# Layer 2's output, layer 3's norm and layer 3's table of messages and keys in one phase of seven node groups

## The reference, cut to what matters

```python
h = jnp.maximum(_layernorm(x), 0.0)
x = x + _L2_gnn_ref(h, edge_index, edge_weight, edge_weight_n2)    # a weighted segment sum
h = jnp.maximum(_layernorm(x), 0.0)
x = x + _L3_gnn_ref(h, ...)

# in _L3_gnn_ref, for an edge of type r from node s:
rel_emb = W_r.mean(axis=-1)[edge_type]                              # 64 values for each of 8 types
key_base = x_src @ Wk1 + rel_emb @ Wk2 + Wk_bias
key_rule = rule_emb[rule_ids] @ Wk3
msg = x_src @ W_r[r]
```

## Time and profile before

| what | us |
|---|---|
| median of 3 runs | 7159.0 |
| lowest and highest | 7148.41 and 7164.03 |
| the profiled execution, its own time | 7143.65 |
| its span in the trace | 7141.9 |
| from the first transpose of `out2` to the first instruction after `table3` | 114.6 (4956.14 to 5070.71) |

### The profile page before, as it was taken

How to read it: one execution, slowest core, us unless ns; L and a number is a source line. 1 busy time by engine, 2 the same in 40 slices (tenths; PEclk the granted TensorE clock), 3 DMA queues, 4 the chain that set the end, 5 groups by cost and what they waited for, 6 DMA issues and landing times. The chain is left out here.

```text
span 7141.9 us, 137103 instructions
## 1 busy us (share of the span) xinstructions
PE 4348.4 (61%) x28781; PEld 2978.7 (42%) x28782; DVE 4343.3 (61%) x20718; ACT 3028.4 (42%) x9954; POOL 5254.0 (74%) x5903
## 2 busy tenths in 40 slices
PE   3343333443356666666666659997777777777774
PEld 2333333333344332323333337776455555555552
DVE  4333333333326666666666679998676666666667
ACT  1000000000004555555555547775466666666663
POOL 6777777777736777777777759997477777777773
PEclk6555555555557767677667679998777777777776
DMA  4333333333325666666666647774533333333331
GB/s 135 100 101 99 103 103 103 101 97 102 103 51 156 169 170 169 170 170 169 169 170 170 169 143 236 240 240 157 189 80 79 79 79 79 79 79 78 79 79 46
DMA packets 657986, 909.22 MB, mean 127 GB/s; under 512 B 141822, under 2 KB 424512, under 8 KB 657537
## 3 DMA queue, kind: packets, MB, share of 16 engines
q1 hardware_dynamic: 480886, 599.15, 26.9%
q0 software_dynamic: 175648, 308.58, 18.8%
q10 hardware_dynamic: 1357, 0.47, 0.0%
HBM read 697.55 MB, written 210.23 MB: 127 GB/s over the span
## 5 line engine op out<-in xcount | busy, mean ns | idle before, releaser
L827 POOL DMA_INDIRECT rows<-src_rows,idx_slots x1568 | 1499.9, 957 | 541.3 <-issue 476.4
L827 POOL DMA_INDIRECT rows<-node_rows,idx_slots x1568 | 1504.2, 959 | 505.9 <-issue 473.9
L827 POOL DMA_INDIRECT rows<-rel_rows,idx_slots x1568 | 1486.1, 948 | 486.3 <-issue 451.6
L1252 PE MATMUL bank<-onehot,ones 128*128 128x512 f32 x1568 | 1242.4, 887 | 10.6 <-ACT onehot L1261 10.6
L1261 ACT ACTIVATE onehot<-ident,fresh_slots 128x128 f32<-128x128 f32 x3136 | 989.3, 386 | 38.4 <-DVE fresh_slots L1388 33.9
L1077 DVE TENSOR_TENSOR wide_room<-bank,wide_room 96x128 f32 x392 | 112.6, 287 | 1326.7 <-PE bank L1055 1326.3
L1041 ACT ACTIVATE rows<-edge_in 128x128 f32<-128x128 f32 x392 | 120.7, 309 | 1836.2 <-PE bank L1055 1820.0
L1349 PE MATMUL bank<-w_e,edge_in 128*128 128x256 f32 x784 | 402.5, 609 | 750.3 <-DVE onehots L906 704.3
L1055 PE MATMUL bank<-onehot,rows 128*96 128x128 f32 x1568 | 390.2, 431 | 628.3 <-issue 328.5
L1055 PE MATMUL bank<-onehots,rows 128*96 128x128 f32 x1568 | 393.9, 433 | 588.7 <-issue 529.7
L1349 PEld LDWEIGHTS bank<-w_e,edge_in 128*128 128x128 f32 x784 | 167.1, 264 | 1248.5 <-DVE onehots L906 782.7
(11 more groups left out here) (274 smaller groups left out, 10192.6 us busy)
## 6 DMA issues: line engine op xcount, KB each, us to landing
edge_in<-dst_line SPq DMA_DIRECT2D x392, 256.0 KB
spill<-rows SPq DMA_DIRECT2D x392, 256.0 KB
rows<-spill SPq DMA_DIRECT2D x392, 256.0 KB, 3.0
hot_rows<-rows SPq DMA_DIRECT2D x98, 712.0 KB, 3.7
onehots<-hot_rows SPq DMA_DIRECT2D x98, 712.0 KB, 4.3
onehots<-src_low SPq DMA_DIRECT2D x98, 512.0 KB, 6.3
edge_in<-in_ea_l SPq DMA_DIRECT2D x98, 256.0 KB, 4.1
rows<-node_rows,idx_slots POOLq DMA_INDIRECT x1568
```

Source lines behind the costliest of these rows:

```text
L827: pool.indirect_dma_start(out=to[:, b.slot(ROW_RING), g, :], out_offset=None, in_=table, in_offset=bass.IndirectOffsetOnAxis(ap=idx_slots[ ...
L1252: return pe.matmul(bank, ones[:, :], diag[:, b.slot(2), :, :].rearrange("p g e -> p (g e)"), start=start, stop=True)
```

## The change

The phases `out2`, `norm3`, `weights3` and `table3` go. One phase `middle3` does the work of `out2`, `norm3` and `table3` in groups of eight tiles: `node_groups` has six of eight and one of two. The derived weights of `weights3` are made in `node_facts_of("norm2")`, with ScalarE copying in place of VectorE, and the mean over the type weights in `head`.

```diff
@@ head, VectorE's last steps
+                c.do(dve.reduce_sum(rel_mean[:, :], w3_rel[0:D, :, :], AX))
+                c.do(dve.tensor_single_scalar(rel_mean[:, :], rel_mean[:, :], 1.0 / D, ALU.mult))
@@ node_facts_of, ScalarE, behind the square root; and TensorE
+                    for n, (to, of) in enumerate((
+                            (rel_bias[:, :], banks[0][0:1, :]),
+                            (rulesT[:, :], banks[1][0:D, 0:N_ACTIVE]),
+                            (rule_keyT[:, :], banks[2][0:D, 0:N_ACTIVE]),
+                            (w3_rule, banks[3][0:D + 1, 0:N_ACTIVE]),
+                            (rel_biases[:, :, :], banks[4][:, :].rearrange(
+                                "p (r o) -> p r o", o=D)))):
+                        act.wait_ge(s_pe, n + 1)
+                        act.activation(to, of, ACT.Copy).then_inc(s_copied, 1)
+                @block.tensor
+                def _(pe):
+                    pe.matmul(banks[0][0:1, :], ones[0:1, 0:1], rel_bias[:, :], start=True, stop=False)
+                    for r in range(N_REL):
+                        last = pe.matmul(banks[0][0:1, r * D:(r + 1) * D], rel_mean[:, r:r + 1],
+                                         w3_k[0:D, 1, :], start=False, stop=(r == N_REL - 1))
+                    last.then_inc(s_pe, 1)
+                    pe.transpose(banks[1][0:D, 0:N_ACTIVE], rules[:, :], ...).then_inc(s_pe, 1)
+                    pe.wait_ge(s_copied, 2)
+                    pe.matmul(banks[2][0:D, 0:N_ACTIVE], w3_k[0:D, 2, :], rulesT[:, :], ...)
+                    pe.wait_ge(s_copied, 3)
+                    pe.matmul(banks[3][0:D + 1, 0:N_ACTIVE], w3_qT[:, :], rule_keyT[:, :], ...)
+                    pe.matmul(banks[4][:, :], ones[0:1, :], rel_bias[:, :], start=True, stop=True)\
+                      .then_inc(s_pe, 1)
@@ new helpers of the phase middle3
+        def centre(dve, c, tiles, s_var):
+            at, av = of_tiles(x, tiles), of_tiles(node_a, tiles)
+            middle, squares = of_tiles(centred, tiles), of_tiles(normed, tiles)
+            wide = [P, len(tiles), D]
+            c.do(dve.reduce_sum(av, at, AX))
+            c.do(dve.tensor_single_scalar(av, av, 1.0 / D, ALU.mult))
+            c.do(dve.tensor_tensor(middle, at, av.unsqueeze(2).to_broadcast(wide), ALU.subtract))
+            c.do(dve.tensor_tensor(squares, middle, middle, ALU.mult))
+            c.do(dve.reduce_sum(av, squares, AX))
+            dve.tensor_scalar(av, av, 1.0 / D, LN_EPS, ALU.mult, ALU.add).then_inc(s_var, 1)
+        def scale(dve, c, t, tiles, s_std, s_normed):
+            dve.wait_ge(s_std, t + 1)
+            inverse = of_tiles(node_b, tiles)
+            c.do(dve.reciprocal(inverse, inverse))
+            dve.scalar_tensor_tensor(of_tiles(normed, tiles), of_tiles(centred, tiles), 0.0,
+                                     inverse.unsqueeze(2)..., ALU.max, ALU.mult).then_inc(s_normed, 1)
+        def root(act, t, s_var, s_std):
+            tiles = node_groups[t]
+            act.wait_ge(s_var, t + 1)
+            act.activation(of_tiles(node_b, tiles), of_tiles(node_a, tiles), ACT.Sqrt)...
+        def turn(pe, t, s_normed, s_feat, s_turned):
+            pe.wait_ge(s_normed, t + 1)
+            for m, tiles in halves(t):
+                if m >= 2:
+                    pe.wait_ge(s_feat, m - 1)
+                for n, j in enumerate(tiles):
+                    last = pe.transpose(banks[2 + m % 2][0:D, n * P:(n + 1) * P], normed[:, j, :],
+                                        ident[:, :])
+                last.then_inc(s_turned, 1)
+        def keep_turned(act, t, s_turned, s_feat):
+            for m, tiles in halves(t):
+                act.wait_ge(s_turned, m + 1)
+                act.activation(featT[0:D, ...], banks[2 + m % 2][0:D, ...], ACT.Copy).then_inc(s_feat, 1)
@@ middle3: TensorE
+                def sums(t):
+                    if t >= 2:
+                        pe.wait_ge(s_taken, t - 1)
+                    (transposes of accT, the group's tiles into banks[t % 2])
+                    last.then_inc(s_out, 1)
+                def table(t):
+                    pe.wait_ge(s_feat, halves(t)[-1][0] + 1)
+                    if t >= 2:
+                        pe.wait_ge(s_key, node_groups[t - 2][-1] + 1)
+                    (keys of all the group's tiles into banks[6 + t % 2])
+                    last.then_inc(s_keys, 1)
+                    for j in tiles:
+                        if j >= 2:
+                            pe.wait_ge(s_message, j - 1)
+                        (messages of tile j into banks[4 + j % 2]).then_inc(s_filled, 1)
+                sums(0)
+                sums(1)
+                for t in range(n_groups):
+                    turn(pe, t, s_normed, s_feat, s_turned)
+                    table(t)
+                    if t + 2 < n_groups:
+                        sums(t + 2)
@@ middle3: VectorE
+                def first(t):
+                    dve.wait_ge(s_out, t + 1)
+                    (x of the group += banks[t % 2]).then_inc(s_taken, 1)
+                    dve.wait_ge(s_taken, t + 1)
+                    centre(dve, c, tiles, s_var)
+                def keys(t):
+                    dve.wait_ge(s_keys, t + 1)
+                    for n, j in enumerate(node_groups[t]):
+                        may_stage(dve, j)
+                        (staged keys of tile j = rel_biases + its keys).then_inc(s_key, 1)
+                first(0)
+                scale(dve, c, 0, node_groups[0], s_std, s_normed)
+                first(1)
+                for t in range(n_groups):
+                    if t + 1 < n_groups:
+                        scale(dve, c, t + 1, node_groups[t + 1], s_std, s_normed)
+                    keys(t)
+                    if t + 2 < n_groups:
+                        first(t + 2)
@@ middle3: ScalarE
+                root(act, 0, s_var, s_std)
+                for t in range(n_groups):
+                    if t + 1 < n_groups:
+                        root(act, t + 1, s_var, s_std)
+                    keep_turned(act, t, s_turned, s_feat)
+                    for j in node_groups[t]:
+                        act.wait_ge(s_filled, j + 1)
+                        may_stage(act, j)
+                        (staged messages of tile j = banks[4 + j % 2]).then_inc(s_message, 1)
```

More of the change, by code:

```diff
@@ L670, in node_facts_of @@
             with Phase(nc, name) as ph:
-                s_chain, s_var, s_std, s_clear = (
-                    ph.sem(n) for n in ("chain", "var", "std", "cleared"))
+                s_chain, s_var, s_std, s_clear, s_pe, s_copied = (
+                    ph.sem(n) for n in ("chain", "var", "std", "cleared", "pe", "copied"))
                 block = ph.open()
@@ new lines, in graph_layers, with of_tiles @@
+        node_groups = [range(g, min(g + 8, NODE_TILES)) for g in range(0, NODE_TILES, 8)]
+        def of_tiles(t, tiles):
+            return t[:, tiles[0]:tiles[-1] + 1]
+        def centre(dve, c, tiles, s_var):
[8 more added lines that the diff above has]
+            dve.tensor_scalar(av, av, 1.0 / D, LN_EPS, ALU.mult, ALU.add).then_inc(s_var, 1)
@@ new lines, in halves @@
+        def halves(t):
+            tiles = node_groups[t]
+            return [(2 * t + n, tiles[4 * n:4 * n + 4]) for n in range(2) if tiles[4 * n:4 * n + 4]]
+        def turn(pe, t, s_normed, s_feat, s_turned):
[7 more added lines that the diff above has]
+                last.then_inc(s_turned, 1)
@@ L1860, in graph_layers @@
         kept_sum_sweep("sum2")
[L1862 to L1871, removed]
@@ L1876, in graph_layers @@
[L1876 to L1920, removed]
@@ L1925, in graph_layers @@
                   for t in (far_in, onehot) for n in range(RING // 2)]
-        with Phase(nc, "table3") as ph:
-            s_filled, s_message, s_key = (ph.sem(n) for n in ("filled", "message", "key"))
+        with Phase(nc, "middle3") as ph:
+            s_out, s_taken, s_chain, s_var, s_std, s_normed, s_turned, s_feat = (
+                ph.sem(n) for n in ("out", "taken", "chain", "var", "std", "normed", "turned",
+                                    "copied"))
+            s_keys, s_filled, s_message, s_key, s_clear = (
+                ph.sem(n) for n in ("keys", "filled", "message", "key", "cleared"))
             s_stored = [ph.sem(f"stored{n}") for n in range(RING)]
             block = ph.open()
+            n_groups = len(node_groups)
             def may_stage(eng, j):
-                eng.wait_ge(s_filled, j + 1)
                 if j >= RING:
@@ L1937, in _ @@
             def _(pe):
[L1938 to L1941, removed]
-                    h = featT[:, j * P:(j + 1) * P]
-                    pe.matmul(banks[RING + j % RING][:, 0:D], h, w3_k[:, 0, :], start=True,
-                              stop=True)
-                    pe.matmul(banks[j % RING][:, :], h, w3_rel[:, :, :].rearrange(
-                        "i r o -> i (r o)"), start=True, stop=True).then_inc(s_filled, 1)
```

(27 more changed lines are left out.)

39 lines of the change are left out of this document (27 added, 12 removed).

## The result

The changed kernel takes 7173.28 us (median of 10 runs, 7164.17 to 7183.32), the kernel before on the same chip 7156.82 (10 runs, 7147.8 to 7164.03). The ratio is 1.0026, interval 1.0018 to 1.0035: slower by 16.5 us, a little over the 0.2% (14 us) that the prediction took as what a measurement can tell. The forecast was 7168, with 7160 to 7178 as its own range.

A forecast was written before the change was run, and what follows sets the result against it. GpSimd, busiest at 74% of the span, is left alone; in the changed stretch the stores decide after the first 43 us. Middle 5.7 us longer plus derived weights 3.1 is 8.8, on 7159.0: 7168, range 7160 to 7178.

The forecast's parts named there:

- First store: Start of the middle stretch: the first store to HBM leaves at 4973.6, 29 us earlier than 5002.7 before.
- Keys and stores: Four-buffer staging ring: tile 8 waits for tile 4's store, at s + 6.4; VectorE's key for it ends s + 7.2.
- `first`: VectorE's norm of a later group, behind `keys` in its stream: 3.95 us, ending s + 11.15, no tile staged meanwhile.
- root and copies: ScalarE: root for the next group 0.30 us, then two copies of this group's transposed tiles at 0.59, ending s + 12.65.
- keys at half clock: TensorE's keys for eight tiles, one block after an idle pause, at clock 0.50: 3.4 us, ending s + 16.05.
- First message: After the keys: 1.08 us on TensorE at full clock, 0.05 and 0.60 on ScalarE, 0.05 to issue: s + 17.85.
- the third rival: TensorE's clock stays half through the messages: cycle 24.4 us, total 7205, slower by 0.65%; chance 0.15 for all or several cycles.
- the first rival: TensorE's clock does not fall in the pauses: keys 1.7 us, cycle 16.2, total 7159; chance 0.14.
- Landing: A group's first store lands 2.6 us after issue, the least seen; at the median, 4.2, five cycles cost 8 us more.
- The root as the wait that decides: ScalarE's stream has `root(t+1)` ahead of `keep_turned(t)`, so group t's copies, keys and messages wait for group t+1's variance.
- Derived weights: `node_facts_of`: ScalarE's copies stand behind its square root, making the phase 3.1 us longer (2.2 to 4), with nothing hiding it.
- overlap to VectorE's bound: Rival: copies don't wait for the next group's root; VectorE bounds at 11.1 us a group, total 7134, 0.35% faster; chance 0.13.

The follow-up runs named there:

- the pause filled: Changed kernel plus six idle TensorE products of 512 columns ahead of the keys in groups 1 to 5; stretch 113.3 us, no whole-kernel time given.
- the weights ahead of the root: Changed kernel with ScalarE's five derived-weight copies ahead of its square root in `node_facts_of`; one execution 7170.51 us, later timed 8680.86 us, ratio 1.0004.
- the copies ahead: Changed kernel with ScalarE's `keep_turned(t)` moved ahead of `root(t+1)`, nothing else; 7134.67 us, ratio 0.9985 to the kernel before.
- the early turn: Changed kernel with ScalarE's copies and derived weights before roots, norm steps between keys, next group's transposes and copies among messages; 7124.09 us, ratio 0.9968 to before.

## Why the prediction was right

Its steps, in their order:

- *First store*: forecast 17.5 us after the first transpose, measured 17.65 (4962.96 to 4980.61).
- *Keys and stores*, *`first`*, *root and copies*, *keys at half clock*: forecast s + 7.2, 11.15, 12.65 and 16.05 (s is the group's first store); measured in the fourth cycle s + 7.25, 11.15, 12.35 and 16.1. The last agrees in part by luck: the root and copies were 0.3 quicker than their term, the keys 0.36 slower. The next key began 2.66 us behind the first store's issue (5039.09 to 5041.75), beside the 2.6 of the earlier trace rows. The prediction's estimate of 3.2, from the Trainium skill's "DMA: Bandwidth & Descriptors", section "Anatomy of one DMA — SWDGE (gpsimd) path", matches none of the six first stores: five at 2.6, one at 5.0. That fit is for GpSimd's DMAs.
- *First message*: this term was mis-sized. The forecast let the clock rise with the keys and took 1.08 and 0.05. The clock was still 0.50, and ScalarE had it 1.82 us behind the keys: 0.7 a cycle, 3.4 in five. It is the third rival in its mildest form. The support that the prediction gave the first rival, that the trace has 0.50 for certain only behind longer pauses, did not fit its own rows: there the clock had fallen 2.8 us behind the last product (5061.7 to 5064.50), and a pause of 5.5 was forecast.
- *Landing*: s + 7.2 for the eighth key held in two cycles (7.4 and 7.25). In the three others it was 9.4, by the late landing, and 7.8 and 8.3, by second messages at half clock: 4.2 us in all. The forecast took the least landing, had the median inside its range, and priced late messages only in the third rival. The cycles add up to 94.1 us instead of 87.5, 6.6 too few: 4.2 here, 3.4 in the first messages and 1.3 in the keys, less 1.5 in root and copies and 0.8 in small terms and in rounding 17.83 up to 17.9. The end, from the sixth group's first store to the next phase, was 16.4 instead of 15.3, another 1.1, and the start 0.2. This is the middle's error, 7.8: 13.5 instead of 5.7.
- *The root as the wait that decides*: shown by moving one line, 29.2 us. The forecast named it as what holds up the copies and all behind them.
- *Derived weights*: 2.45 instead of 3.1 (its terms add up to 3.0). The small copies took 0.15 and 0.17, partly under hand-overs; the bias row's broadcast took 2.07, as forecast.
- *Head*: nothing, as forecast. VectorE's last step moved from 47.73 to 48.66, the next phase begins at 58.12 in both:

```profile
48.66 0.22 DVE L603 TENSOR_TENSOR w_qv<-w_qv,v_mean 67x64 f32<-67x64 f32 x1
...
58.12 1.07 DVE L1149 TENSOR_SCALAR onehot<-iota,dst_rel 128x128 f32<-128x128 f32 x5 [9.24 <-PEq L190]
```

- *Sum*: 8.8 forecast, 15.9 in the two phases, 16.5 between the medians. The time, 7173.28, is inside the own range, 5.3 above the forecast. That is partly luck: the base, 7159.0 from three runs, was 2.2 above the median of ten, and the change itself, 8.8 instead of 16.5, was forecast too small by nearly half. The sign was that of the likeliest case. Its "within 0.2%" was missed narrowly: the ratio is 1.0026, with an interval from 1.0018, and slower by over 0.2% had a chance of 0.24.

Of the rivals, that the clock does not fall was priced at 16.2 a cycle, and with the pause filled it is 16.0. Overlap to VectorE's bound, 11.1 a group, came true only where the order was changed in the streams of TensorE, VectorE and ScalarE (cycles of 10.6 to 12.2).

## What to carry to other kernels

In a loop over groups shared by five in-order streams, write each stream's order down and ask for every wait what stands behind it: a root for the next group ahead of this group's copies cost 29 us of 127 here, 11 to 12 of them by the clock. Price a burst after a pause at half clock through to the first result that someone waits for, not through its first block only. Where an engine idles in every cycle, first try to move work into the pause, and see by the stretch's length, not by its busy share, whether the pause was on the path.

## What the runs showed of the hardware that was not expected

With the middle as after, a store of 512 KB issued into an empty queue was waited for 2.6 us in all groups but the second, and there 4.96, 4.38, 4.41 and 4.37 us in the four traces (after, its repeat, the weights ahead of the root, twice). In each of the four a 16 KB instruction packet was in the DMA engines while the store's last part was outstanding; with the pause filled it came 2.5 us ahead of the store, and the wait was 2.6. TensorE worked 8.1 us on end at 0.50 (5013.80 to 5021.90), where the earlier trace rows had it back at 1.00 behind 3.3 and 3.5 us; and its clock fell from 1.00 while TensorE worked, in the sixth group's keys, both after and with the copies ahead. A sweep of 750 us was 757 to 764 us long in the four traces with a reordering in the phase ahead of it; the cause is open. One kernel, the early turn, took 7124 us at one time and, but for one order in the facts phase, 8645 at a later one, 21% more, with the middle as long in both (87.0 and 86.3 us): what grew is GpSimd's idle time ahead of its gathers of rows, from 543 to 1189, 505 to 755 and 487 to 1048 us, nearly all of the difference. Why is open.
